# Row loads issued by SyncE: 32 ready-made byte offsets per register load, and 17 tiles a layer instead of 12

## The reference, cut to what matters

```python
h = relu(layernorm(x))
for l in range(2):
    xn = layernorm(h); xp = xn + xn @ Wpos[l] + deg[:, None] * Wdeg[l] + ...
    q, k, v = xp @ Wq[l], xp @ Wk[l], xp @ Wv[l]              # (3125, 128) each
    att = clip(sum_d(q[dst] * k[src]) / 4, -50, 50)            # one number a head and edge
    alpha = softmax of att over the edges with the same dst
    h = h + segment_sum(v[src] * alpha, dst) @ Wo[l]
    h = h + gelu(layernorm(h) @ W1[l]) @ W2[l]
out = x + h
```

## Time and profile before

| | us |
|---|---|
| median of 3 runs | 2160.54 (2155.23 to 2160.68) |
| the profiled execution, its own time | 2156.61 |
| its span | 2154.9 |
| POOL busy | 1547.5 (72% of the span) |
| DVE busy | 1712.5 (79%) |
| PE busy | 1408.5 (65%) |
| ACT busy | 940.0 (44%) |

### The profile page before, as it was taken

How to read it: one execution, slowest core, us unless ns; L and a number is a source line. 1 busy time by engine, 2 the same in 40 slices (tenths; PEclk the granted TensorE clock), 3 DMA queues, 4 the chain that set the end, 5 groups by cost and what they waited for, 6 DMA issues and landing times.

```text
span 2154.9 us, 42066 instructions
## 1 busy us (share of the span) xinstructions
PE 1408.5 (65%) x8227; PEld 1229.6 (57%) x8227; DVE 1712.5 (79%) x5151; ACT 940.0 (44%) x2179; POOL 1547.5 (72%) x1645
## 2 busy tenths in 40 slices
PE   4865566666766676666676667676665757566666
PEld 4655555555655565655556556565555656555555
DVE  8758798889898978787876777787777777787775
ACT  8333353353535353533554335344343535344344
POOL 7177777777777777777727777777777777777773
PEclk9979788788888888787978778779787877878787
DMA  2365445444444444444424444444444444444441
GB/s 89 114 183 157 151 143 158 144 142 146 138 143 137 145 135 136 137 144 136 135 67 141 129 137 136 141 128 141 137 140 127 141 138 126 141 136 141 127 141 54
DMA packets 128957, 289.94 MB, mean 135 GB/s; under 512 B 34596, under 2 KB 63200, under 8 KB 128704
## 3 DMA queue, kind: packets, MB, share of 16 engines
q0 software_dynamic: 76672, 209.16, 33.7%
q1 hardware_dynamic: 52032, 78.08, 11.0%
HBM read 275.44 MB, written 8.38 MB: 132 GB/s over the span
## 4 chain that ended last, share of the span: by engine, by line
POOL 35%; issue 20%; DVE 16%; PE 15%; ACT 7%; DMA 3%; SPq 2%; DVEq 1%; ACTq 0%
POOL kvr L842 35%; PE bank L1120 5%; DVE agg L1756 5%; PE bank L1133 4%; DVE kvr L1363 2%; DVE prod L1716 2%; DMA kvr<-kv_table,srcidx 2%; ACT apart L1320 2%; ACT onehotT L1324 1%; DVE onehot L1708 1%; SPq L698 1%; PE bank L1077 1%; ACT L1279 1%; PE bank L857 1%; ACT L1330 1%
## 5 line engine op out<-in xcount | busy, mean ns | idle before, releaser
L842 POOL DMA_INDIRECT kvr<-kv_table,srcidx x1588 | 1506.3, 949 | 543.2 <-issue 473.6
L1120 PE MATMUL bank<-q,onehotT 128*128 x3320 | 607.1, 340 | 697.0 <-DVE prod L1716 369.6
L1120 PEld LDWEIGHTS bank<-q,onehotT 128*128 128x128 f32 x3320 | 517.5, 238 | 807.2 <-issue 806.0
L1133 PE MATMUL bank<-msg,onehot 128*128 128x136 f32 x3320 | 601.9, 340 | 2.6 <-DVE msg L1743 1.9
L1330 ACT ACTIVATE bank<-attc 128x32 f32<-128x32 f32 x404 | 81.2, 201 | 1114.3 <-DVE attc L1737 1111.3
L1133 PEld LDWEIGHTS bank<-msg,onehot 128*128 128x128 f32 x3320 | 561.8, 248 | 5.5 <-DVE msg L1743 3.7
L1756 DVE TENSOR_TENSOR agg<-agg,bank 128x136 f32 x1624 | 469.2, 289 | 60.3 <-PE bank L1133 53.1
L1716 DVE TENSOR_TENSOR prod<-kvr,bank 128x512 f32<-128x512 f32 (+1 forms) x404 | 272.4, 674 | 221.7 <-DMA kvr<-kv_table,srcidx 173.5
L1320 ACT ACTIVATE apart<-relT,minus_p 128x512 bf16<-128x512 bf16 x416 | 293.9, 706 | 6.7 <-DMA relT<-rel_table 6.3
L1743 DVE TENSOR_TENSOR msg<-kvr,bank 128x512 f32<-128x512 f32 (+1 forms) x404 | 270.8, 670 | 16.8 <-ACT bank L1330 16.6
L1708 DVE TENSOR_TENSOR onehot<-bank,rel 128x512 f32<-128x512 f32 x416 | 282.6, 682 | 0.4
(11 more groups left out here) (219 smaller groups left out, 859.4 us busy)
## 6 DMA issues: line engine op xcount, KB each, us to landing
relT<-rel_table SPq DMA_DIRECT2D x104, 512.0 KB
rowkv<-kv_table SPq DMA_DIRECT2D x3072, 1.0 KB
kvr<-kv_table,srcidx POOLq DMA_INDIRECT x1588
loop_kv<-kv_table SPq DMA_DIRECT2D x25, 128.0 KB
kv_table<-qkv SPq DMA_DIRECT2D x25, 128.0 KB
kv_table<-onehot SPq DMA_DIRECT2D x8, 256.0 KB, 2.2
w<-weights SPq DMA_DIRECT2D x2, 840.0 KB, 7.6
loops<-x_in SPq DMA_DIRECT2D x5, 320.0 KB, 5.3
```

Of the source, the lines that this page charges most:

```text
L842: pool.indirect_dma_start(kvr[:, n % RING, j, :], None, kv_table[l], bass.IndirectOffsetOnAxis(ap=srcidx[:, step:step + 1], axis=0)).then_ ...
L1120: mm = pe.matmul(bank[2][:, j * D:(j + 1) * D], onehotT[:, m % OHT, j, :], q[:, bass.ds(ranks[j + h], 1), :].rearrange("p a c -> p (a c)") ...
L1133: mm = pe.matmul(sum_ps(n, k), onehot[:, m % OH, j, :], msg[:, n % 2, j, :], start=(m, j) == of[0], stop=(m, j) == of[-1])
```

## The change

Before, 12 tiles a layer (groups 24, 40, ..., 200) are loaded by SP, 8 rows in each of 16 slots; now 17 tiles (groups 19, 30, ..., 195), 11 or 12 rows in each of 11 slots. POOL gathers 1578 tiles instead of 1588. POOL makes one new table, `srcbyte`, in which each source node stands as the byte offset of its row (node number times 1024); SP loads 32 of these at once into registers, and the DMA's source is given as bytes, so that the register is used as it is. The 12 small DMAs that brought node numbers into `srcrow`, and the waits around them, are gone.

```diff
-ROWS_A_SLOT, ROWS_LEAD, ROW_BUFS = 8, 3, 3
-ROW_SLOTS = -(-P // ROWS_A_SLOT)
+ROW_SLOTS, ROWS_A_LOAD, ROWS_LEAD, ROW_BUFS = 11, 32, 3, 3
 ROWED = [tuple(range(first + ROW_SLOTS + ROWS_LEAD, GROUPS - 1, ROW_SLOTS)) for first in (5, 5)]
-ROW_STEPS = sorted({g for rowed in ROWED for g in rowed})
+ROW_BYTES = KV * 4
...
-        srcrow = sb("srcrow", [1, len(ROW_STEPS) * P], I32)
+        srcbyte = sb("srcbyte", [P, SC * P], I32)
...
-            sp.wait_ge(s_rows, 16 * 2 * SC)
-            for i, g in enumerate(ROW_STEPS):
-                chunk, step = divmod(row_of(g, at_begin=True) + G - 1, P)
-                sp.dma_start(srcrow[0:1, i * P:(i + 1) * P], step_src[step:step + 1, chunk * P:(chunk + 1) * P]).then_inc(s_srcrow, 16)
-
...
-            sp.wait_ge(s_srcrow, 16 * len(ROW_STEPS))
...
                 if part == 0:
+                    if i == 0:
+                        sp.wait_ge(s_srcbyte, 1)
...
-                p0 = part * ROWS_A_SLOT
-                at = ROW_STEPS.index(g) * P + p0
-                nodes = nc.values_load_multi_w_load_instructions(srcrow[0:1, at:at + min(ROWS_A_SLOT, P - p0)], engines=(ENG.SP,), min_val=0, max_val=NP - 1,
-                                                                 skip_runtime_bounds_check_because="the number of a node")[1]
-                for j, node in enumerate(nodes):
-                    sp.dma_start(rowkv[p0 + j:p0 + j + 1, i % ROW_BUFS, :], kv_table[l][bass.ds(node, 1), :]).then_inc(s_rowkv[i % ROW_BUFS], 16)
+                chunk, step = divmod(row_of(n, at_begin=True) + G - 1, P)
+                table = kv_table[l].rearrange("(a r) c -> a (r c)", a=1).bitcast(U8)
+                for p in range(P * part // ROW_SLOTS, P * (part + 1) // ROW_SLOTS):
+                    if p % ROWS_A_LOAD == 0:
+                        at = chunk * P + p
+                        nodes[:] = nc.values_load_multi_w_load_instructions(srcbyte[step:step + 1, at:at + ROWS_A_LOAD], engines=(ENG.SP,), min_val=0, max_val=(NP - 1) * ROW_BYTES,
+                                                                            skip_runtime_bounds_check_because="the place of a node's row in the table")[1]
+                    sp.dma_start(rowkv[p:p + 1, i % ROW_BUFS, :].bitcast(U8), table[:, bass.ds(nodes[p % ROWS_A_LOAD], ROW_BYTES)]).then_inc(s_rowkv[i % ROW_BUFS], 16)
...
             pool.wait_ge(s_rows_f, 3)
+            pool.tensor_scalar(srcbyte[:], step_src_f, float(ROW_BYTES), None, ALU.mult).then_inc(s_srcbyte, 1)
             pool.tensor_copy(rel_bf, step_dst_f).then_inc(s_rel_bf, 1)
```

More of the change, by code:

```diff
@@ L514, in build @@
         s_kv = [sem(f"s_kv{r}") for r in range(RING)]
-        s_srcrow = sem("s_srcrow")
+        s_srcbyte = sem("s_srcbyte")
         s_rowkv = [sem(f"s_rowkv{u}") for u in range(ROW_BUFS)]
@@ L678, in _ @@
                     sp.dma_start(x[:, bass.ds(r, 1), :], x_nat[:, b0 + j:b0 + j + 1, :]).then_inc(s_x_ranked, 16)
+            nodes = []
             def fetch_rows(l, g, part):
```

## The result

The changed kernel takes 2183.8 us in the median of 4 runs (2182.3 to 2185.71), against 2160.61 us (2155.23 to 2165.83) for the kernel before in 4 runs beside it: a ratio of 1.0103, 95% interval 1.0087 to 1.0119. The profiled execution's own time is 2184.56 us and its span 2182.8, so 28 us more than the profiled one of before on either count.

The account below looks back on a forecast made before the run. Gathers were taken to set the pace in layer 1 and late in layer 0, with SP becoming the bound in layer 0 after the change. 2156.6 + 29 (layer 0) - 6 (layer 1) = 2180 us; range 2146 to 2240.

Parts of the forecast that it names:

- What bounds, and how full SP is: Gathers set the pace throughout layer 1, late in layer 0; SP's only slack is 56.7 us and 103.8 us of waits.
- The row: One row load on SP, without FUSED_REGOPS and one gap of three: 0.336 us in place of 0.412.
- The register load: One SP load of 32 values: 2.10 us (0.78 to 3.12), plus 0.14 for dispatch and longer first rows.
- the trip per value: Rival: each value of SP's register loads pays its own trip, 310 ns; a tile 83 us, kernel 3220 us; chance 0.03.
- The tile: SP's work for one row tile: 128 rows and four register loads, 52.0 us in place of 67.5.
- The rivals: SP keeps pace, 2144 us, 0.27; in between, 2150 to 2163, 0.13; both layers SP bound, 2302, 0.13; trip per value, 0.03.
- the forecast's own case: SP bound in layer 0 alone, a tile of 51.0 to 53.2 us: 2163 to 2205 us, chance 0.44.
- the first rival: SP keeps the pace, rows come when the gathers do, for instance a row at 0.32 us: 2144 us, chance 0.27.
- The last row of layer 0: SP's clock: start 149.2, 884 of rows, 64 of other loads and stores, 5 of waiting; issued at 1102 us.
- That the last row sets the end of layer 0: Group 195's rows come 29 us late against before, and nothing behind that group gives this back.
- Layer 0: The layer where SP's rows come late and the consumer waits for them: +29 us.
- The costs put at nothing: POOL's new operation, 2.9 us ahead of idle time; DVE's split operations, 3 us, under gathers or rows; row loads' data, nothing.

## Why the prediction was right, step by step

**What bounds, and how full SP is**: right. In layer 1 five tiles more gain what their gathers save, and in either layer tiles beyond SP's slack lose about what SP lacks. The other theories fell: the addressing alone changes nothing, more tiles in layer 1 alone are a gain, and moving `x0` alone gives back half of layer 0's loss.

**The row**, predicted 0.336 us (0.257 to 0.375): the median distance of two row DMAs, which was to be near it, is 0.322 (0.412 before). One instruction and its gap went, as taken, and 14 ns more.

**The register load**, predicted 2.10 us and 0.14 beside it: 2.175, and 0.33 beside it, which is what a tile takes beyond 128 rows of 0.322 and four loads. The form of the price was right, so much for a value and so much once. The Trainium skill (Runtime: NRT & Kernel Launch, Instruction fetch mechanics) gives about 200 ns a register even for bulk loads, and has the loads in view that the runtime adds. The kernel's own loads from SBUF pay 68 ns a value at 32; the estimate worked out from that sentence, 2750 us, is 566 us too high, and the trip per value, 3220, more than 1000.

**The tile**, predicted 52.0 us: 51.3, from all records of lines 695 and 697 in layer 0 added up (871 us for 17 tiles); 128 x 0.332 + 4 x 2.215 gives 51.4. The rivals began from 51.0 downward and from 53.2 upward, so the forecast's own case held, by 0.3 us a tile, and with luck: the row at 0.32 us that the first rival named for its example all but came true (1.8 us a tile less), and only what a tile takes beside its plain rows (1.1 us more than taken) made up for more than half of it.

**The last row of layer 0**, predicted 149.2 + 884 + 64 + 5 = 1102 us: 1101.4, but by errors that cancel. The first register load started at 152.3 (+3), 17 tiles took 871 (-13), the waits 5.1, and what is left for `relT`, `x0`, self loops and stores is 73 (+9). By the tile alone layer 0 would have grown by only 17; the step that was mis-sized is that remainder, which I had carried over from before as the rest of a subtraction and never read by itself. It had hardly changed: before, the 12 tiles took 801 us by their records and not 810 (one cycle of 17.32 us stood for all), so the remainder was 74 and not 67.

**That the last row sets the end of layer 0**: not so. It was issued 4 us before DVE came for it, and group 195 does not wait. DVE's last wait for rows in layer 0 is at group 184, at 1051.51, and ACT's last one for `relT` ends at 1031.5; from there on the consumer runs at its own pace. The forecast let the lateness pile up to the last tile; in fact 35.1 us were there at group 118 and no more came: SP's last row tiles of the layer followed each other at 53.5 us in the mean, and there 11 groups of before had taken 53.6. That the end of the layer came out within 4 us all the same is in part luck.

**Layer 0**, predicted +29: +32.0 at the first gather of layer 1, of which 1.9 us are a later first gather (100.12 against 98.25), which I had not counted. This delay starts ahead of POOL's new operation, and the kernel with `x0` late, which has this operation too, begins at 98.7; so I don't put it down to the change, but its cause is open. The wait at group 19, predicted some 9 us, was 6.6. `relT` came late and POOL waited for the ring, both as predicted.

**Layer 1**, predicted -6: -4.3 in the profiled execution, and -6.3 (-4.1 to -8.4) by the ratio of the kernel with 17 tiles in layer 1 alone.

**The costs put at nothing**: POOL's new operation (line 821) takes 3.60 us where 2.9 were allowed, and 20.17 us of idle time still stand behind it in POOL's timeline of the changed kernel, so its cover held:

```profile
50.78 3.60 POOL L821 TENSOR_SCALAR srcbyte<-onehotT 128x896 int32<-128x896 f32 x1
...
75.56 2.94 POOL L826 MEMSET agg<- 128x3400 f32 x1 [20.17 <-PE bank L923]
```

DVE's split operations lie under the gathers in layer 1, since that layer gained.

**The sum**, 2180: 2183.8 in the median, where the profiled execution, against which the sum was made, went from 2156.61 to 2184.56; +28 for +23.

Open is how the 35 us up to group 118 divide between SP's two late products. DVE's waits for rows there are 35.1 us where before they were 10.4, ACT's for `relT` 14.7 and 6.3, but not all of ACT's need reach DVE. Loading `relT` by another queue would tell, and was not tried.

## What to carry to other kernels

An engine that only issues has no busy time on the page: add up what it must issue in each stage, and set it against the time that the pace maker of that stage needs, stage by stage. Making such an engine cheaper gives nothing by itself, and handing it more work pays only up to the end of its slack, here 1.255 us a gather on the one side and 51 us of SP a tile on the other. Beyond it most of what is added counts: with loads of 16 the last row of layer 0 came 27.7 us later and layer 0 took 27.8 us longer, and with `x0` moved the row came 16 us earlier and the layer took 11 us less. Before loading it to the brim, look for what else stands in its queue and can stand elsewhere: the 25 `x0` loads, moved behind the last group, gave back some 14 us.

## What the hardware showed that I had not expected

The register loads of the row tiles lie nearly on a straight line in the number of values: medians of 781 ns for 8, 1003 for 12, 1257 for 16 and 2175 for 32, that is 55 to 64 ns for each further value and about 0.3 us once. Two loads of 16 are thus 0.34 us dearer than one of 32, which is the once-paid part again; in this kernel that alone, eight loads a tile in place of four, was worth 38 us. The line doesn't hold for every load on SP: four values at line 596 took 304 ns, and two or three at line 608 took 931 in the median and 283 at the least, so the number of values is not all that counts.
